# Another order of the operations between two batches, and of the three products of each value group

## The reference, cut to what matters

```python
inp = x + 2.0 * sinu
q = conv2d(inp, wq)            # 1x1
k = conv2d(inp, wk, 1, 1)      # 3x3
v = conv2d(inp, wv, 1, 1)      # 3x3
q, k, v = split_heads(q), split_heads(k), split_heads(v)     # 8 heads of 32, 1024 tokens
q = q * cos + rotate_every_two(q) * sin
k = k * cos + rotate_every_two(k) * sin
dots = jnp.einsum('bhid,bhjd->bhij', q, k) * SCALE
attn = jax.nn.softmax(dots, axis=-1)
attn = jnp.einsum('bhij,hg->bgij', attn, mix)
out = jnp.einsum('bhij,bhjd->bhid', attn, v)
o = conv2d(out, wo) + bo[None, :, None, None]
a, g = jnp.split(o, 2, axis=1)
return a * jax.nn.sigmoid(g)
```

## Time and profile before

| what | value |
|---|---|
| median of the runs | 2935.95 us |
| the profiled execution | 2935.72 us, its span 2934.0 us |
| mean granted TensorE clock | 0.979 |
| TensorE busy | 2783.5 us (95%) |
| VectorE busy | 2266.9 us (77%) |
| ScalarE, GpSimd busy | 1468.7 us, 1396.2 us |
| one convolution stage of batches 1 to 7 | 54.5 to 57.7 us |
| one main stage of batches 1 to 7 | 256.3 to 257.6 us |

### The profile page before, as it was taken

How to read it: one execution, slowest core, us unless ns; L and a number is a source line. 1 busy time by engine, 2 the same in 40 slices (tenths; PEclk the granted TensorE clock), 3 DMA queues, 4 the chain that set the end, 5 groups by cost and what they waited for, 6 DMA issues and landing times.

```text
span 2934.0 us, 51178 instructions
## 1 busy us (share of the span) xinstructions
PE 2783.5 (95%) x20238; PEld 2607.3 (89%) x20238; DVE 2266.9 (77%) x3470; ACT 1468.7 (50%) x1884; POOL 1396.2 (48%) x1055
## 2 busy tenths in 40 slices
PE   6999999999999999999999999999999999958996
PEld 5999889998999899989999899989998999847776
DVE  6777788778877897788877887788778977655663
ACT  3455445553555355534554455535553555446771
POOL 4344533553455534553464335444455346347883
PEclk9999999999999999999999999999999999879998
DMA  2555020102010210102110301020101103037665
GB/s 110 200 200 210 15 90 23 34 22 94 22 40 27 76 41 24 43 34 72 30 41 9 104 23 33 24 94 23 39 28 69 47 24 100 8 135 265 233 225 205
DMA packets 88792, 230.01 MB, mean 78 GB/s; under 512 B 17160, under 2 KB 17746, under 8 KB 88566
## 3 DMA queue, kind: packets, MB, share of 16 engines
q1 hardware_dynamic: 79478, 209.96, 21.4%
q0 software_dynamic: 9088, 16.94, 1.8%
HBM read 90.76 MB, written 96.89 MB: 64 GB/s over the span
## 4 chain that ended last, share of the span: by engine, by line
PE 72%; DVE 9%; POOL 7%; issue 6%; DMA 3%; ACT 3%; SPq 1%; POOLq 0%; DVEq 0%; ACTq 0%
PE PV L711 46%; PE ST L711 12%; PE MX L711 12%; POOL yrows L677 3%; POOL acc L590 1%; DVE rt L1425 1%; DMA wt<-wall 1%; DMA stk<-rt 1%; DMA qst<-stk 1%; ACT xr L1106 1%; DVE El L1461 1%; PE PV L819 1%; DVE tmp L1440 1%; POOL rt L583 1%; DVE ul L1379 1%
## 5 line engine op out<-in xcount | busy, mean ns | idle before, releaser
L590 POOL TENSOR_TENSOR acc<-acc,tmp 128x256 f32<-128x256 f32 x512 | 802.2, 1567 | 1201.0 <-DVE tmp L1471 1198.7
L711 PE MATMUL PV<-vh,El 128*128 128x258 f32 x4096 | 1186.7, 290 | 10.3 <-DVE El L1461 5.2
L711 PE MATMUL PV<-vh,Eh 128*128 128x258 f32 x4096 | 1157.3, 283 | 0.0
L711 PE MATMUL PV<-vl,Eh 128*128 128x256 f32 x4096 | 1148.3, 280 | 0.0
L1106 ACT ACTIVATE Eh<-ST 128x1024 fp32r<-128x1024 f32 x512 | 525.7, 1027 | 732.8 <-PE ST L711 732.8
L1456 DVE TENSOR_REDUCE mcol<-MX 128x1 fp32r<-128x1024 f32 x512 | 625.8, 1222 | 271.9 <-PE MX L711 271.4
L711 PEld LDWEIGHTS PV<-vh,El 128*128 128x128 f32 x4096 | 772.6, 189 | 43.6 <-issue 11.4
L711 PEld LDWEIGHTS PV<-vl,Eh 128*128 128x128 f32 x4096 | 779.7, 190 | 24.7 <-issue 3.8
L711 PEld LDWEIGHTS PV<-vh,Eh 128*128 128x128 f32 x4096 | 774.1, 189 | 0.0
L1461 DVE TENSOR_TENSOR El<-E,Eh 128x1024 fp32r<-128x1024 f32 x512 | 641.6, 1253 | 0.4
L1106 ACT ACTIVATE E<-ST 128x1024 f32<-128x1024 f32 x512 | 521.9, 1019 | 0.0
(11 more groups left out here) (244 smaller groups left out, 3375.0 us busy)
## 6 DMA issues: line engine op xcount, KB each, us to landing
rows<-xr SPq DMA_DIRECT2D x68, 520.0 KB, 6.1
stk<-rt SPq DMA_DIRECT2D x64, 512.0 KB, 2.8
kst<-stk SPq DMA_DIRECT2D x192, 128.0 KB
qst<-stk SPq DMA_DIRECT2D x192, 128.0 KB
wt<-wall SPq DMA_DIRECT2D x39, 514.0 KB
wt<-wall SPq DMA_DIRECT2D x39, 512.5 KB
xrow<-rows SPq DMA_DIRECT2D x39, 260.0 KB
wall<-yrows SPq DMA_DIRECT2D x32, 256.0 KB, 4.7
```

The costliest lines, as they stand in the source:

```text
L590: nc.gpsimd.tensor_tensor(acc[:, ic, :], acc[:, ic, :], tmp[:, p, :], ALU.add).then_inc(s_acc, 1)
L711: return nc.tensor.matmul(o, w, m, start=start, stop=stop)
```

## The change

Two things are changed. In `values` the three matmuls of each key block no longer stand together: for a piece of 2 or 4 key blocks all high by high products come first, then all high by low (`Eh` by `vl`), then all low by high (`El` by `vh`). The wait for `exp_lo` (`s_lo`) moves from the first matmul of the piece to its first low product, and the first matmul waits for the exponentials (`s_ex`) in its place. The first piece of a pair of heads waits for `vh` (`s_vhi`) at its start and for `vl` (`s_vlo`) before its `vl` products. The other part moves steps in the three lists of the convolution stage. No operation is added or dropped.

```diff
-            def values(n, k, p, jcs):
+            def values(n, k, p, jcs, low=None):
                 e = k % 2
+                hi, lo = ([t[:, e, jc, p * P:(p + 1) * P] for jc in range(KC)] for t in (Eh, El))
                 for jc in jcs:
                     if jc == 0:
                         wait(pe, s_nrm, 2 * n + p + 1)
                     if p == 0 and jc % 4 == 0:
+                        wait(pe, s_ex, 2 * n + jc // 4 + 1)
+                    mm(PV[p][:, 0:VW], hi[jc], vh[:, jc, :], jc == 0, False)
+                if low is not None:
+                    pe.wait_ge(s_vlo, low)
+                for jc in jcs:
+                    mm(PV[p][:, 0:INNER], hi[jc], vl[:, jc, :], False, False)
+                for jc in jcs:
+                    if p == 0 and jc % 4 == 0:
                         wait(pe, s_lo, 2 * n + jc // 4 + 1)
-                    hi, lo = (t[:, e, jc, p * P:(p + 1) * P] for t in (Eh, El))
-                    mm(PV[p][:, 0:VW], lo, vh[:, jc, :], jc == 0, False)
-                    mm(PV[p][:, 0:INNER], hi, vl[:, jc, :], False, False)
-                    last = mm(PV[p][:, 0:VW], hi, vh[:, jc, :], False, jc == KC - 1)
+                    last = mm(PV[p][:, 0:VW], lo[jc], vh[:, jc, :], False, jc == KC - 1)
...
                 conv_q(b, 0)
                 conv_q(b, 1)
+                conv_q(b, 2)
+                conv_q(b, 3)
                 if prev is not None:
                     out_transpose(prev, 0)
-                conv_q(b, 2)
-                conv_q(b, 3)
                 conv(b, 0, 0)
+                conv(b, 0, 1)
                 if prev is not None:
                     out_transpose(prev, 1)
-                conv(b, 0, 1)
-                if prev is not None:
                     out_project(prev, 0)
...
                 conv(b, 1, 2)
+                conv(b, 1, 3)
                 if prev is not None:
                     out_project(prev, 1)
-                conv(b, 1, 3)
                 conv(b, 2, 0)
+                conv(b, 2, 1)
+                conv(b, 2, 2)
                 if prev is not None:
                     route_in(prev)
-                conv(b, 2, 1)
-                conv(b, 2, 2)
                 conv(b, 2, 3)
...
+                max_scores(n + 1, 1, 0)
                 scores(n, 0, 0, b)
-                max_scores(n + 1, 1, 0)
                 conv(b, 3, 3)
+                max_scores(n + 1, 1, 1)
                 scores(n, 0, 1, b)
-                max_scores(n + 1, 1, 1)
```

On ScalarE `middle_copy(b, 0)` moves from the second place to behind `gate_tanh(prev, 0)`, `rot_hi(b, 5)` ahead of `gate_tanh(prev, 1)`, and `rot_hi(b, 7)` ahead of `v_hi(b, 1)`. On VectorE `rotate(b, 1)` moves ahead of `out_lo(prev, 0)`, `clear` behind `rotate(b, 2)`, `gate(prev, 0)` ahead of `rot_lo(b, 2)`, `out_lo(prev, 1)` and `even_odd(b, 0, 1)` ahead of `turn(b, 4)`, `take_max` ahead of `rot_lo(b, 7)`, and:

```diff
                 middle_sums(b, 1)
-                if prev is not None:
-                    gate(prev, 1)
                 rot_lo(b, 4)
                 even_odd(b, 1, 0)
                 even_odd(b, 1, 1)
                 rot_lo(b, 5)
                 turn(b, 6)
+                if prev is not None:
+                    gate(prev, 1)
                 turn(b, 7)
```

More of the change, by code:

```diff
@@ L912, in pair @@
                 if split is not None:
-                    wait(pe, s_vlo, split)
+                    wait(pe, s_vhi, split)
                 for k in range(2 * QC):
@@ L917, in pair @@
                     for p in range(2):
-                        values(n, k, p, range(0, 2))
+                        values(n, k, p, range(0, 2), split if k == 0 and p == 0 else None)
                         if p == 0 and not (last and k == 7):
@@ L1218, in batch @@
                     out_hi(prev, 0)
-                middle_copy(b, 0)
                 rot_hi(b, 0)
@@ L1223, in batch @@
                     gate_tanh(prev, 0)
+                middle_copy(b, 0)
                 rot_hi(b, 2)
@@ L1229, in batch @@
                 rot_hi(b, 4)
+                rot_hi(b, 5)
                 if prev is not None:
                     gate_tanh(prev, 1)
-                rot_hi(b, 5)
                 middle_copy(b, 2)
@@ L1237, in batch @@
                 v_hi(b, 0)
+                rot_hi(b, 7)
                 v_hi(b, 1)
-                rot_hi(b, 7)
                 middle_copy(b, 3)
@@ L1623, in batch @@
                 rotate(b, 0)
+                rotate(b, 1)
                 if prev is not None:
                     out_lo(prev, 0)
-                rotate(b, 1)
+                rot_lo(b, 0)
+                rotate(b, 2)
                 if prev is not None:
                     clear(prev)
-                rot_lo(b, 0)
-                rotate(b, 2)
                 rot_lo(b, 1)
@@ L1634, in batch @@
                 even_odd(b, 0, 0)
-                rot_lo(b, 2)
                 if prev is not None:
                     gate(prev, 0)
+                rot_lo(b, 2)
+                even_odd(b, 0, 1)
+                if prev is not None:
+                    out_lo(prev, 1)
                 turn(b, 4)
                 rot_lo(b, 3)
-                if prev is not None:
-                    out_lo(prev, 1)
-                even_odd(b, 0, 1)
                 turn(b, 5)
                 middle_sums(b, 1)
-                if prev is not None:
-                    gate(prev, 1)
                 rot_lo(b, 4)
@@ L1651, in batch @@
                 turn(b, 6)
+                if prev is not None:
+                    gate(prev, 1)
                 turn(b, 7)
                 middle_sums(b, 2)
+                rot_lo(b, 6)
                 even_odd(b, 2, 0)
@@ L1656, in batch @@
                     logits(prev)
-                rot_lo(b, 6)
                 v_lo(b, 0)
+                take_max(n, 0, 0)
+                rot_lo(b, 7)
                 even_odd(b, 2, 1)
-                take_max(n, 0, 0)
+                take_max(n, 0, 1)
                 v_lo(b, 1)
-                rot_lo(b, 7)
-                take_max(n, 0, 1)
                 middle_sums(b, 3)
```

## The result

The changed kernel takes 2921.98 us, the median of six runs (2919.39 to 2927.19), beside 2937.65 us for the kernel before on the same chip: a ratio of 0.9946, with a 95% interval from 0.9935 to 0.9957. That is 15.7 us, 0.54%. On another chip it took 2925.18 us against 2934.75, 0.9964 [0.9950, 0.9978]. The forecast was 2905 us, a gain of 31 us, with a range from 2892 to 2922. The sign was right, half of the gain is not there, and the time stands at the upper edge of the range.

What follows compares the result with a forecast made beforehand. TensorE, busy 95% of the span, was taken as the bound; removed waits and regained clock summed to 27.6 us, plus 2 for restarts, giving 2906 from 2935.7, put at 2905 us; range 2892 to 2922.

Steps and rivals of the forecast that it cites:

- so I leave it at 979.18: Transposes of the last batch's sums, batch 3: GpSimd's addition hangs on VectorE's last divisions, so their start does not move.
- T: Transposes of the last batch's sums: two more `conv_q` ahead cover most of the wait for GpSimd, 9.6 us.
- D: First head's operands from memory: data come 3.9 us earlier, TensorE 1.6, so most of the wait goes, 10.5 us.
- L: TensorE's waits for `El` in the main stage: products ahead of the first low one cover most, 1.5 us.
- from there to the end of `rot_lo(b, 5)` VectorE takes 18.46 us: VectorE's stretch from `middle_sums(b, 0)`: without the gate's 2.48 us, moved behind it, the data come 2.5 us earlier.
- P: Pace of the 12,288 reordered value products on TensorE: no change, 0, between -7 and +7 us.
- O: Write of `out_lo(prev, 1)` moves ahead of `turn(b, 4)`: TensorE's wait for it goes, 1.5 us.
- Rival (1): VectorE in the convolution stage gives the gain back, `middle_copy(b, 0)` tying it to TensorE: 2925 us, chance 0.13.
- C: Clock in three long convolution stages: half speed goes with the late data, 4.5 us.
- E: Stage end after `conv(b, 3, 3)`: VectorE's chain keeps the 6.1 and 3.6 us of waits, gain 0.
- only the value products had such neighbours: Argument for the rival that value products with differing neighbour weights run slower: 2955 us at 4 ns each, chance 0.04.

Runs made afterwards that it cites:

- its undoing: Changed kernel with `conv_q(b, 2)` and `(b, 3)` put back behind `out_transpose(prev, 0)`: 2937.54 us, 1.0008 of the kernel before.
- the lists alone: Changed kernel's convolution-stage lists with the value products in their old order: 2919.14 us against 2936.82 for the kernel before, 0.9945.
- the value order alone: New order of the value products put into the kernel before, its convolution-stage lists unaltered: 2943.33 us, 1.0020 of the kernel before.
- with the gate back: Changed kernel with `gate(prev, 1)` back ahead of `rot_lo(b, 4)` on VectorE: 2946.23 us, 1.0040 of the kernel before.
- the version with the gate between the two turns and the old value products: Changed kernel with PSUM-reading VectorE instructions beside GpSimd's turns, gate between `turn(b, 6)` and `turn(b, 7)`, old value order: 2914.42 us, 0.9934 of the kernel before.
- the two versions with all covers: Changed kernel, PSUM-reading VectorE instructions at four places beside GpSimd's turns, gate behind `turn(b, 7)`: 2933.24 us with new value order, 2926.16 with old.
- the small kernel: Separate kernel, VectorE multiplying 128x512 alone and beside GpSimd: both operands in SBUF 0.69 and 1.74 us, one in PSUM 0.68 in both.
- once its work is cut: Changed kernel with GpSimd's two instructions of groups 4 to 7 on 64 of 512 columns: 2908.48 us, 0.9901 of the kernel before.
- With both lifted: Changed kernel with GpSimd's instructions of groups 4 to 7 on 64 of 512 columns and value products in threes, `El` last: 2899.17 us, 0.9877 of kernel before.

## Why the prediction was wrong

Two of its steps failed, and a term with them. The first step is "so I leave it at 979.18", the transposes 3.42 us behind the first `conv_q`: it was taken from the kernel with the old value order. With the new one they stand 4.33 us behind it, since TensorE comes to its first `conv_q` earlier (in batch 3 2.23 us behind VectorE's `xl` instead of 3.15) and GpSimd's last addition does not (4.01 us behind it in both kernels); T and the start of D were counted from that place, and L was to gain there. The second is "from there to the end of `rot_lo(b, 5)` VectorE takes 18.46 us", less the gate: durations were carried into another order as if they were the instruction's own, and the stretch took 16.7 us where 15.98 were counted, with two more instructions of 1.3 and 1.76 us behind it. The term is P, put at nothing: it is 6.7 us.

- **T** held by itself: 9.4 us by its undoing, and 9.6 in the lists alone (12.9 to 3.3 us), 9.6 forecast. But the wait at the transposes fell only from 12.9 to 10.0 us in the changed kernel, because of L.
- **L** failed. The waits for `El` go (3.9 us), but the value order alone raised the wait at the transposes by 6.5 us. "What is gained there is waited for again at the transposes" was written down, and then 1.5 us were counted all the same; these two waits together grew by 2.6.
- **O** held: the 1.5 us for `out_lo` are gone, and no other wait came for them at `out_project`.
- **D** failed in half. The wait for memory fell by 9.3 us (10.5 forecast), but waits of about 1.1 us for `mcol` in four stages and 0.4 in a fifth came in its place, and 1.8 us for `xg`. VectorE ended `rot_lo(b, 5)` 31.4 us behind the first `conv_q` (969.30 to 1000.71), where it took 33.4 before: 2.0 us earlier and not 3.9. Of the missing 1.9 us, 1.1 lie in the start, `middle_sums(b, 0)` at 14.70 us and not at 13.6, which is the value order's again (13.75 without it). The other 0.7 are the pace: the stretch took 16.7 us (984.00 to 1000.71) where 15.98 were counted, since durations depend on what GpSimd does beside them. Rival (1), "VectorE gives it back", was the right worry with another cause: `middle_copy(b, 0)` was done 0.3 us before VectorE came to `middle_sums(b, 0)`.
- **C** failed: 4.5 us forecast, nothing came. Half clock left the three long stages, and with the gate back it followed the long wait for memory in all seven, so the step from that wait to half clock has support (though in the version with the gate between the two turns and the old value products two waits of about 2 us had none behind them). But four stretches of it stand in the changed trace as before. Three are at the start of main stages behind waits of 0.40, 0.54 and 0.40 us, and the fourth comes where TensorE had waited no more than 0.3 us at a time since the transposes. Why these waits cost the clock in batches 1, 4 and 7 and not in the others stays open.
- **E** held: `vt`, `vl` and `mcol` have 1.34 us at the end of batch 3's stage, and before the two kinds there had 9.7 in seven, 1.39 a stage.
- **P** was put at 0 between -7 and +7, and is +6.7: the upper end. The rule of the Trainium skill that was set aside there ("TensorE: Matmul & The Clock Gate", section "Step-by-step: what each phase is for") points the right way, if the shared `Eh` block is the reason; but the price is 6.7 us, where the estimate by the Trainium skill's figure was 437. Against "only the value products had such neighbours": the two matmuls of `max_scores` share a block of `qst` too, in both kernels.

Each cause is shown by itself: the value order by its loss of 6.5 us alone and by the 7.1 us between the two versions with all covers, GpSimd by the small kernel and by `turn` at 0.69 us once its work is cut. With both lifted the whole forecast is there. How much of those 36 us belongs to which is not shown: that run also shortens GpSimd's own chain, and the half clock is gone from it. Nor do the terms close. To the end of the seventh main stage the listed waits fall by 12.1 us in the changed kernel (46.4 to 34.3), the pace takes 5.9 of it back, and these batches became 11.6 us shorter: some 5 us of gain stand in no wait of the list, where 2 were counted for restarts.

## What to carry to other kernels

When instructions are moved, their durations aren't constants: look up for each what the other engines did beside it before, and what they will do beside it now. Instructions on VectorE that read PSUM are the ones to put where GpSimd works in SBUF, as long as nothing that TensorE waits for comes later by it: the covers at four places lost their gain to the gate. And a wait removed ahead of a fixed point is a gain only once that point moves.

## What the runs showed of the hardware

Beside GpSimd, a VectorE multiplication of 128x512 with both operands in SBUF took 1.74 us instead of 0.69; with one operand in PSUM 0.68 in either case. Value products grouped by kind ran 0.026 us a unit of 48 slower than in threes by key block, in either order of the kinds. And waits of 1.2 to 1.5 us in the middle of a stage were followed by half clock (0.74 over 13 us in one of them) in five stages of seven, the same waits in the other two by none.
